# The first image of the second attention: where its numerators are loaded, how its inverses are spread, and where v is computed

## The reference, cut to what matters

```python
# x: (4, 48, 48, 128); N = 2304 tokens per image, 8 heads of 16 channels
q, k, v = gn(x) @ Wq + bq, (gn(x) @ Wk + bk) * d ** -0.5, gn(x) @ Wv + bv
lepe    = depthwise_conv5x5(v) + dw_b
attn    = rotate(q) @ rotate(k)^T + mask             # per head, 2304 x 2304
out     = softmax(attn) @ v + lepe
x       = x + out @ Wo + bo
t = x;  l = layernorm(t)                             # second attention, one head of 128
t = t + softmax((l@Wq1+bq1) @ (l@Wk1+bk1)^T) @ (l@Wv1+bv1)
t = t + ffn_with_top2_experts(layernorm(t))
```

## Time and profile before

| | |
|---|---|
| median of 3 runs | 3610.34 us (3608.89 to 3616.03) |
| profiled execution | 3615.75 us, span 3614.0 us |
| TensorE matmul / weight load busy | 95% / 73% of the span |
| VectorE / ScalarE / GpSimd busy | 73% / 56% / 45% |
| mean granted TensorE clock | 0.976 of full |
| DMA | 309.5 MB, mean 86 GB/s |

### The profile page before, as it was taken

One profiled execution on the slowest core, in us unless ns is written; L12 is line 12 of the kernel. 1 busy time (PEld: TensorE's weight loads), 2 busy tenths in 40 slices (PEclk: granted clock), 3 DMA queues, 4 the chain that ended last, 5 costly groups with the idle time before them and its releaser, 6 DMA issues. The chain is left out here.

```text
span 3614.0 us, 96388 instructions
## 1 busy us (share of the span) xinstructions
PE 3426.4 (95%) x30672; PEld 2653.5 (73%) x30672; DVE 2623.8 (73%) x6490; ACT 2029.5 (56%) x3660; POOL 1639.8 (45%) x854
## 2 busy tenths in 40 slices
PE   6599999999999999999999999999399999999988
PEld 4377777777777777777777777777277787877867
DVE  6588888888888888888888888888365564644457
ACT  3366666666666666666666666666145444454533
POOL 4565566565665565556655656566100100005112
PEclk9799999999999999999999999999699999999989
DMA  6732242224224224223322322221511020100011
GB/s 201 243 101 93 91 125 78 93 98 129 67 100 126 94 66 135 91 94 93 109 91 98 103 94 91 99 68 63 167 42 56 24 74 6 37 1 1 1 41 42
DMA packets 111321, 309.50 MB, mean 86 GB/s; under 512 B 11496, under 2 KB 72859, under 8 KB 90299
## 3 DMA queue, kind: packets, MB, share of 16 engines
q1 hardware_dynamic: 111195, 307.85, 27.4%
HBM read 253.49 MB, written 54.31 MB: 85 GB/s over the span
## 5 line engine op out<-in xcount | busy, mean ns | idle before, releaser
L747 DVE CUSTOM_DVE_ANT_0 c_S<-c_Sps,mask_tiles 128x768 f32<-128x768 f32 x1728 | 1619.5, 956 | 425.1 <-PE c_Sps L798 367.0
L688 ACT ACTIVATE c_PT<-c_Tps 128x512 f32<-128x512 f32 x2592 | 1428.7, 605 | 872.0 <-PE c_Tps L809 809.4
L659 POOL TENSOR_SCALAR c_S<-c_S,c_row_max 128x2304 f32<-128x2304 f32 x576 | 1410.9, 2450 | 949.4 <-DVE c_row_max L758 949.4
L809 PE MATMUL c_Tps<-ident,c_S 128*128 128x128 f32 x10368 | 1399.5, 273 | 4.1 <-ACT c_PT L688 4.1
L809 PEld LDWEIGHTS c_Tps<-ident,c_S 128*128 128x128 f32 x10368 | 1226.0, 140 | 151.4 <-ACT c_PT L688 9.9
L798 PE MATMUL c_Sps<-c_K,c_Q 96*128 (+1 forms) x3456 | 853.5, 328 | 43.5 <-DVEq L728 26.3
L822 PE MATMUL c_Ops<-c_PT,c_V 128*32 128x256 f32 x10368 | 619.1, 382 | 0.8 <-ACT c_PT L688 0.8
L822 PEld LDWEIGHTS c_Ops<-c_PT,c_V 128*32 128x32 f32 x10368 | 307.4, 109 | 243.7 <-issue 49.9
L798 PEld LDWEIGHTS c_Sps<-c_K,c_Q 96*128 96x128 bf16 x3456 | 315.0, 98 | 202.7 <-issue 144.4
L1313 DVE TENSOR_SCALAR_CACHE_REDUCE l_S<-l_Sps 128x384 f32<-128x384 f32 x432 | 240.2, 557 | 294.5 <-PE l_Sps L1161 268.2
L1081 ACT ACTIVATE ln2T<-l_Tps 128x384 f32<-128x384 f32 x432 | 196.4, 491 | 403.9 <-PE l_Tps L1182 403.9
(11 more groups left out here) (197 smaller groups left out, 1652.2 us busy)
## 6 DMA issues: line engine op xcount, KB each, us to landing
mask_tiles<-in_mask SPq DMA_DIRECT2D x144, 1152.0 KB, 7.7
numerators<-c_O SPq DMA_DIRECT2D x288, 64.0 KB
ln<-numerators SPq DMA_DIRECT2D x8, 2304.0 KB, 8.4
q_parts<-f_parts SPq DMA_DIRECT2D x12, 576.0 KB, 7.7
k_parts<-f_parts SPq DMA_DIRECT2D x12, 576.0 KB
c_Q<-q_parts SPq DMA_DIRECT2D x71, 96.0 KB
c_vpad<-v_padded SPq DMA_DIRECT2D x8, 756.0 KB, 14.8
c_K<-k_parts SPq DMA_DIRECT2D x7, 864.0 KB, 8.8
```

The costliest lines, as they stand in the source:

```text
L659: pool.tensor_scalar(S[:, slot, :], S[:, slot, :], -1.0, row_max[:, slot:slot + 1], ALU.mult, ALU.add).then_inc(shifted, 1)
L688: act.activation(dst, src, ACT.Exp, scale=-1.0).then_inc(exp_done, 1)
L747: dve.tensor_tensor_reduce(out=S[:, r % ROW_SLOTS, cols(CH, c)].rearrange("p (k n) -> p k n", k=2), in0=Sps[:, n % S_SLOTS, :, 0:GW], in1= ...
L809: last = pe.transpose(Tps[:, g % T_SLOTS, cols(P, k)], S[:, (2 * b + t) % ROW_SLOTS, cols(P, kt)], ident[:, :])
```

## The change

It touches image 0 of the second attention alone, and the SyncE list for the others where it must.

- The mask's memory and `ln2` become one buffer that is never freed. `first_num` is a view of it: for each half of the tokens four numerators of 1152 columns, so that half 0 is pair 70's mask tiles and half 1 is pair 71's.
- In `layer0_core` SyncE stores pair 70 before the conv's last half, loads half 0 of image 0's numerators when pair 70's scores have been taken, and seven heads of half 1 when all scores have; head 7's sixteen channels of half 1 (its last pair reaches them) are loaded after the last store has landed, as the block's last instruction.
- The weights and bias rows are loaded from ScalarE's queue. On SyncE's queue the order is denominators, conv, store of the inverses, the eight rows of inverses (`inv8`, one partition per head), x.
- TensorE spreads the inverses: six products of an 8 x 128 matrix of zeros and ones (`spread`, built by eight small GpSimd instructions) with `inv8`, into the PSUM buffers of the scores; VectorE multiplies the summed numerators with them from PSUM, three groups of 384 columns per half, then adds conv and its bias.
- `project` starts its groups 0 to 2 when half 0 of z is there, and 3 to 5 when half 1 is.
- `to_v` and `take_v` of image 0 stand behind `scores(0, 0)` and `take_scores(0, 0)`; TensorE's wait for VectorE's takes of v then stands ahead of `scores(0, 1)`.
- For image 1 SyncE's loads begin when image 0's projection has been computed (`o_ready`), since they go to the memory of `first_num`; the loop over images is written out instead of being a loop of the engine.

```diff
@@ layer0_core, SyncE
+            store_pair(PAIRS - 2)
+
+            def load_first(half, channels):
+                sp.dma_start(first_num[channels, half, :, :],
+                             s["o_load"][0][channels, :, cols(N // 2, half)]).then_inc(first_in[half], 16)
+
+            sp.wait_ge(s_taken, ROWS * NCH * (PAIRS - 1) + S_SLOTS)
+            load_first(0, slice(0, C))
             store_half(HEADS - 1)
-            store_pair(PAIRS - 2)
+            sp.wait_ge(s_taken, ROWS * NCH * PAIRS + S_SLOTS)
+            load_first(1, slice(0, C - D))
             store_pair(PAIRS - 1)
             sp.wait_ge(conv_stored, 16 * (HEADS + 2))
             sp.wait_ge(o_stored, 16 * STORES * (PAIRS + 2))
+            load_first(1, slice(C - D, C))
@@ layer1_attention, SyncE
             sp.dma_start(den[:, :, :], s["den_load"][0]).then_inc(den_in, 16)
-            for i, w in enumerate(("Wo0", "Wq1", "Wk1", "Wv1")):
-                sp.dma_start(weights[:, i, :], a[w]).then_inc(weights_in, 16)
-            for i, w in enumerate(("bo0", "bq1", "bk1", "bv1")):
-                sp.dma_start(rows[:, i, :], a[w].rearrange("(a n) -> a n", a=1)).then_inc(weights_in, 16)
-            load_half(0, 0)
-            spread_inverses(0)
             sp.dma_start(conv[:, :], s["conv"][0]).then_inc(conv_in, 16)
-            sp.wait_ge(half_taken, 1)
-            load_half(0, 1)
+            store_inverses(0)
+            sp.dma_start(inv8[:, :], s["inv_load"][0]).then_inc(inv8_in, 16)
             load_x(0)
-            with sp.Fori(1, B) as i:
-                sp.wait_ge(z_ready, i)
+            for i in range(1, B):
+                if i == 1:
+                    sp.wait_ge(o_ready, NG)
+                else:
+                    sp.wait_ge(z_ready, i - 1)
                 sp.dma_start(den[:, :, :], s["den_load"][i]).then_inc(den_in, 16)
                 load_half(i, 0)
                 sp.dma_start(conv[:, :], s["conv"][i]).then_inc(conv_in, 16)
                 sp.wait_ge(var_ready, i)
                 load_x(i)
-                spread_inverses(i)
-                sp.wait_ge(half_taken, 2 * i + 1)
+                store_inverses(i)
+                sp.dma_start(z[:, :], s["inv_load"][i].unsqueeze(1).to_broadcast([HEADS, D, N])).then_inc(inv_in, 16)
+                sp.wait_ge(half_taken, 2 * i - 1)
                 load_half(i, 1)
@@ GpSimd
+            for h in range(HEADS):
+                last = pool.tensor_scalar(spread[:, cols(D, h)], ones[:, 0:D], ident[0:HEADS, h:h + 1], None, ALU.mult)
+            last.then_inc(constants, 1)
@@ ScalarE
+            for i, w in enumerate(("Wo0", "Wq1", "Wk1", "Wv1")):
+                act.dma_start(weights[:, i, :], a[w]).then_inc(weights_in, 16)
+            for i, w in enumerate(("bo0", "bq1", "bk1", "bv1")):
+                act.dma_start(rows[:, i, :], a[w].rearrange("(a n) -> a n", a=1)).then_inc(weights_in, 16)
@@ TensorE
-            pe.wait_ge(constants, 2)
+            pe.wait_ge(constants, 3)
...
+            pe.wait_ge(inv8_in, 16)
+            for g in range(NG):
+                if g >= S_SLOTS:
+                    pe.wait_ge(wide_taken, g - S_SLOTS + 1)
+                pe.matmul(Sps[:, g % S_SLOTS, 0:GW], spread[:, :], inv8[:, cols(GW, g)], start=True, stop=True).then_inc(wide_ready, 1)
...
-            project(0, 0)
+            project(0, 0, first=True)
             transpose_ln(0, 0)
             to_q_or_k(0, NG, first=True)
             to_q_or_k(1, 2 * NG)
-            to_v(NG)
-            projected(T_PREP, O_PREP)
+            pe.wait_ge(t_taken, T_PREP + T_SLOTS)
             scores(0, 0, 0)
+            to_v(NG)
+            pe.wait_ge(o_taken, O_PREP + O_SLOTS)
@@ VectorE
+            def finish_first(half):
+                dve.wait_ge(first_sum, 2 * half + 2)
+                for k in range(NG // 2):
+                    g = half * (NG // 2) + k
+                    part = first_num[:, half, 0, cols(GW, k)]
+                    dve.wait_ge(wide_ready, g + 1)
+                    dve.tensor_tensor(part, Sps[:, g % S_SLOTS, 0:GW], part, ALU.mult).then_inc(wide_taken, 1)
+                dve.wait_ge(wide_taken, (half + 1) * (NG // 2))
+                if half == 0:
+                    dve.wait_ge(conv_in, 16)
+                part = first_num[:, half, 0, :]
+                dve.scalar_tensor_tensor(out=part, in0=part, scalar=conv_bias[:, :], in1=conv[:, cols(HN, half)],
+                                         op0=ALU.add, op1=ALU.add).then_inc(first_z, 1)
...
+            sum_first_pairs(0)
             invert(0)
-            sum_half(0, 0)
+            sum_first(0)
...
-            finish_half(0, 0)
-            sum_half(0, 1)
-            finish_half(0, 1)
+            sum_first_pairs(1)
+            sum_first(1)
+            finish_first(0)
+            finish_first(1)
...
-            take_v(0, NG)
             dve.wait_ge(t_taken, T_PREP + T_SLOTS)
             stage(0, 0, 0)
             stage(0, 1, 1)
             take_scores(0, 0, 0, None)
+            take_v(0, NG)
```

More of the change, by code:

```diff
@@ L879, in _, with layer1_attention @@
                 values(PAIRS - 1, 1, group)
[L882 removed]
+def layer1_attention(nc, a, s, ident, conv_bias, x1, ln2, ln2T, sums, first_num, first_in):
     with ExitStack() as ctx:
@@ L1112, in _, with project @@
             pe.matmul(Tps[:, 1, C:2 * C], ones[0:1, :], rows[0:1, 3, :], start=True, stop=True).then_inc(small_ready, 1)
+            pe.wait_ge(inv8_in, 16)
[3 more added lines that the diff above has]
+                pe.matmul(Sps[:, g % S_SLOTS, 0:GW], spread[:, :], inv8[:, cols(GW, g)], start=True, stop=True).then_inc(wide_ready, 1)
             pe.wait_ge(small_taken, 3)
-            def project(i, n):
-                pe.wait_ge(z_ready, i + 1)
+            def project(i, n, first=False):
+                if not first:
+                    pe.wait_ge(z_ready, i)
                 for g in range(NG):
+                    if first and g % (NG // 2) == 0:
+                        pe.wait_ge(first_z, g // (NG // 2) + 1)
                     pe.wait_ge(o_taken, n + g + 1)
                     for k in range(GB):
-                        last = pe.matmul(Ops[:, g % 2, cols(P, k)], z[:, cols(P, g * GB + k)], weights[:, 0, :],
-                                         start=True, stop=True)
+                        tokens = first_num[:, g // (NG // 2), 0, cols(P, (g % (NG // 2)) * GB + k)] if first else z[:, cols(P, g * GB + k)]
+                        last = pe.matmul(Ops[:, g % 2, cols(P, k)], tokens, weights[:, 0, :], start=True, stop=True)
                     last.then_inc(o_ready, 1)
@@ L1243, in sum_half @@
             def sum_half(i, half):
-                dve.wait_ge(half_in, 16 * (2 * i + half + 1))
+                dve.wait_ge(half_in, 16 * (2 * i + half - 1))
                 for x in (0, 2):
@@ L1789, in hybrid @@
         conv_bias = ctx.enter_context(nc.sbuf_tensor("conv_bias", [P, 1], F32))
+        ln2 = ctx.enter_context(nc.sbuf_tensor("mask_tiles", [P, B * TILES, C], F32))
+        mask = ln2[:, :, :].rearrange("p t c -> p (t c)").rearrange("p (i n) -> p i n", i=4)
+        first_num = ln2[:, :, :].rearrange("p t c -> p (t c)").rearrange("p (f j n) -> p f j n", f=2, j=4)
+        first_in = [ctx.enter_context(nc.semaphore(f"first{half}_in")) for half in range(2)]
         stages12 = ctx.enter_context(ExitStack())
-        mask = stages12.enter_context(nc.sbuf_tensor("mask_tiles", [P, 4, N], F32))
         K = stages12.enter_context(nc.sbuf_tensor("c_K", [KR, 2 * B * N], BF16))
```

41 lines of the change are left out of this document (22 added, 19 removed).

## The result

The changed kernel takes 3587.68 us in the median of four runs (3586.16 to 3589.26) against 3612.63 (3608.89 to 3616.03) for the kernel before on the same chip: a ratio of 0.9931, 95% interval 0.9914 to 0.9948, 25.0 us faster. The forecast was 3583.2, range 3577 to 3591. The span of the first profile is 3587.5, 26.5 less than before.

The account below looks back on a forecast made before the run. The join between the two attentions waits for a chain of transfers ending in x with its bias. Gains of 26.3 + 2.0 - 1.2 = 27.1 us took the median from 3610.34 to 3583.2 us, range 3577 to 3591.

Parts of the forecast that it names:

- the store home: In the join, the store of the inverses lands 1.9 us after issue, where it had taken 7.57.
- part three: Image 0's v placed behind the first scores in the second attention: no gain, 1.2 us lost.
- the denominators, 3.33: In the join, from the denominators' issue to VectorE's start: 2.83 plus 0.5 for head 7 ahead and the weights beside.
- The small products: TensorE's small products in the join, put at ending at 2559.5 where they ended at 2558.34 before.
- the bias 14 to 15 us behind the denominators' issue: Sign in the join's profile: GpSimd's bias on x starts that long after the denominators' load is issued, and ends last.
- the 2.0 for the clock: Image 0's projection takes 4.74 us instead of 6.77, the spreading keeping TensorE busy at the fast clock: 2.0 us gained.
- sign of 24.5 us from the first q product to the transposes: Sign in the second attention's start: this stretch of image 0 takes 24.5 us instead of 23.3.
- The 3.9 us by which the bias came last: In the kernel before, x with its bias, not the numerators, ends the chain before the projection, by 3.9 us.
- the low end: Fastest total time, 3577 us: v hiding, a bias of 5.77, denominators landing 0.5 sooner, runs 1.5 below their median.
- The low clock: Rival: TensorE's clock stays low through the projection, so the 2.0 us are not gained; 3585 us, chance 0.24.
- The inverse store: Rival: the store of the inverses waits 7.57 us as at the join, not 1.9; 5.7 more, 3589 us, chance 0.08.
- The tiles kept their pace: Against the rival that attention tiles run at 1.2 GHz, about 20 us instead of 10.15; four give 3624, chance 0.02.

Follow-up runs that it names:

- e1: The changed kernel with v of image 0 computed ahead of the first scores again; 3588.47 us (one time).
- e11: The changed kernel itself measured once more on another occasion; median 3589.32 us, ratio 0.9936 to the kernel before.
- e2: The kernel before with only v of image 0 moved behind the first scores; 3612.98 us (one time).
- e7: The changed kernel with GpSimd signalling each of its six bias additions, VectorE waiting only for the group it takes; 3584.74 us (one time).
- e4: The changed kernel with both halves of the numerators loaded behind the denominators at the second attention's start; 3596.45 us (one time).
- e3: The changed kernel with the inverses loaded onto 128 rows by one transfer, TensorE spreading nothing; 3600.59 us (one time).
- e5: The changed kernel with head 7's load moved behind the denominators, into the second attention's block; 3591.37 us (one time).
- e9: The changed kernel with v first, bias by groups, second half's sums earlier, and small transfers first on SyncE's queue, conv and x last; median 3584.69 us, ratio 0.9927.
- e10: As e9, with 30 dummy transposes ahead of TensorE's small products and 22 ahead of the spreading; median 3583.16 us, ratio 0.9919.
- e8: The changed kernel with v first, bias by groups, second half's sums earlier, head 7 and x behind the denominators, conv behind the inverses; 3588.14 us, ratio 0.9933.
- e6: The changed kernel with 44 unused identity transposes on TensorE ahead of the small products; 3588.97 us (one time).

## Why the prediction was right

By its own steps, each against the first profile of the changed kernel:

| step | forecast us | measured us |
|---|---|---|
| head 7's issue | 0.45 | 0.32 (5.17 from the last copy to the denominators' issue, 4.85 before) |
| denominators to VectorE | 3.33 | 4.96 |
| adding, inverting, issue | 2.03 | 1.98 |
| the store home | 1.9 | 2.33 |
| issue of the eight rows | 0.5 | 0.35 |
| x to GpSimd | 6.50 | 6.71 |
| the bias | 7.99 | 8.02 |
| gain to the end of the bias | 26.3 | 24.3 |
| gain in the projection | 2.0 | 2.2 here; 0.3 in e1, 0.9 in e11 |
| v behind the scores | -1.2 | -1.4, and -1.4 in e1 and e2 |

**Right:** that x with its bias sets the end and keeps setting it; that VectorE's chain stands about 1 us behind (0.85; e7 took the bias away and gained 1.2); that the early loads cost nothing where they were put (the last pair is no later with them, and e4, which puts them back, loses 9.2 us); that the broadcast, with what queues behind it, was the larger part (e3: 11.5 us; the two were each undone alone, so the sizes need not add up); that part three is a loss and why; that the bias loses its 2 us to the two conv additions alone (8.02, as in the join before: two of its six instructions took 2.1 us, each beside a conv addition, the other four 1.0).

**Off in size:** the term "the denominators, 3.33", which measured 4.96 and makes up 1.6 of the 2.0 us by which the chain was too short; the store home adds 0.4. I allowed 0.5 for head 7 ahead and the weights beside. e5 shows that head 7 alone costs about 1.1; in e9 and e10, where weights and head 7 stand behind the denominators in one queue and conv comes later still, it is 3.08 and 2.83 again. What the remaining 0.9 of e5 is, weights on the other queue or conv, wasn't separated. The small products, put at 2559.5, were off as well: counted from the landing of the last stores they ended 3.7 us later than that. On ScalarE's queue the last bias row took 5.7 us from issue to TensorE's start, 2562.30; on SyncE's, before, it took 1.2. This stayed hidden only because the bias was late too: VectorE waited 3.11 us for these products, so with the denominators on time its chain would have ended last, at about the 23.50 us where it did, and of the 2.0 us under 1 would have come back (an estimate from the changed kernel's timeline). One of the signs, the bias 14 to 15 us behind the denominators' issue, was missed for the same reason: 16.33.

**Right in size, wrong in kind:** the 2.0 for the clock. I argued that the spreading would keep TensorE busy and so bring the clock up. It doesn't; at 2576 it was still 0.50. The clock came up in the middle of the projection, 3.4 us after its start as in e3 without any spreading, and the same instructions had 6.51 us in e1. That the term came out at 2.2 is luck. Also by chance the kernel before had been profiled with 9.80 us for q and k, where the twelve other profiles have 8.01 (its clock was still 0.50 when they began); that is 1.8 us of the 27 that no part of the change earned. (The prediction's sign of 24.5 us from the first q product to the transposes carries it: the changed kernel has 22.93.) These two made up for the late denominators. Taking typical values instead (projection 6.7 before, from its profile and e2's, and 5.9 after, the mean of the five profiles that share its order: 4.54, 6.51, 6.51, 5.88, 5.86), 24.3 + 0.8 - 1.4 gives **23.7 us**, and the medians moved by 25.0 and 23.1. Against the 27.1 of the forecast that is 3.4 too little: 2.0 from the chain, 1.2 from the clock, 0.2 from part three. The median of 3587.68 lies 4.5 above 3583.2, and of that 2.3 are only that the kernel before measured 3612.63 this time instead of 3610.34. The mechanism of the chain held; that of the clock didn't.

Two readings of the prediction want a correction. The 3.9 us by which the bias came last in the kernel before are VectorE's idle time up to its first take; from the end of its conv addition (2596.98) to the end of the bias it is 3.7, and TensorE's first two groups ended only 0.7 ahead of the bias (2599.98). And the terms of the low end add up to 3577.9, not 3577.

None of the rivals came true in full. The low clock did in part. The inverse store was 0.4 late in the changed kernel and 4.5 to 5.2 us home in e5 and e8, where more stood ahead of it: the rival was the right thing to fear when the order is changed. The tiles kept their pace.

## What to carry to other kernels

When a stall is a chain of dependent transfers, list what stands ahead of each link in its queue. A small transfer on the chain belongs ahead of the bulk, and moving one big load only passes the wait to the next link, as e5 and e8 show and e9 avoids. Once the chain is cut, the second-latest input is the new end; here it was 0.85 us away. Taking the bias out of the way alone gained 1.2 us (e7), and moving x ahead of the inverses made the end of VectorE's chain 0.8 later (e8). And put work behind other work "to hide it" only if the engine has idle time there: TensorE had none, so the new order only laid bare two semaphore waits. When a forecast rests on one profile, look whether its stretch is typical; 1.8 us of the kernel before were not.

## What the runs showed that I had not expected

- In no profile did TensorE's clock come up during its products over 8 rows: it was full for 8.04 us on end in e8, at 0.50. It came up during identity transposes over 128 rows, within 5 us (e6).
- The moment at which the clock comes up differs between executions of the same instructions: 4.54, 6.51 and 5.86 us for the same six groups in the changed kernel, e1 and e11, and with no spreading ahead 3.3 us after the projection's start in e3. That one profile can be 2 us off its kernel's mean in such a stretch is what e3's and e4's times have to be read with.
- Eight GpSimd instructions on 8 by 16 numbers took 2.41 us with VectorE waiting (e4), 4.73 in the changed kernel, and 6.10 beside VectorE's sums in e9.
- The last bias row took 5.7 us on ScalarE's queue, with conv's 1152 KB issued on SyncE's queue 3 us ahead of it, against 1.2 on SyncE's queue in the kernel before. Queue and bulk weren't told apart.
